# Fewer and larger weight loads, weight reductions behind the attention group, and memory loads issued after the stage before them

## The reference

```python
q, k, v = x @ w_q.T, x @ w_k.T, x @ w_v.T
sigma_q = elu(q) + 1
a_mem = einsum('bsd,mde->mbse', sigma_q, memories)
raw   = einsum('bsd,md->mbs', sigma_q, memory_norms)
w     = softmax(raw.mean(axis=-1), axis=0)
mem_out = einsum('mbse,mb->bse', a_mem / clip(raw, 1e-6)[..., None], w)
out = g * mem_out + (1 - g) * causal_attention(q, k, v)      # 16 heads of 128
x = layernorm(x + out @ w_o.T)
h = relu(bitlinear(x, w_up)) ** 2                            # 2048 -> 4096
x = layernorm(x + bitlinear(h, w_down))                      # 4096 -> 2048
```

## Time and profile before

| | |
|---|---|
| median of 3 runs | 3046.87 us (3042.25 to 3052.11) |
| the profiled execution | 3053.26 us |
| its span on the slowest core (core 7) | 3051.7 us |
| spans of the eight cores | 3004.0 to 3051.7 us |
| TensorE busy / VectorE / ScalarE / GpSimd | 74% / 37% / 23% / 9% of the span |
| read from memory / written | 294.23 MB / 8.39 MB |

### The profile page before, as it was taken

The page is one execution under the profiler, slowest core; times in us unless marked ns, Lnnn a source line. Parts: engine busy times, 40 slices in busy tenths (PEclk is TensorE's granted clock), DMA queues, the critical chain, the costliest instruction groups (busy, mean ns, idle before and its releaser), DMA issues.

```text
span 3051.7 us, 37968 instructions; the slowest of 8 cores (3004.0 to 3051.7 us)
## 1 busy us (share of the span) xinstructions
PE 2263.3 (74%) x14858; PEld 1450.8 (48%) x14858; DVE 1136.6 (37%) x1393; ACT 713.5 (23%) x1232; POOL 287.2 (9%) x453
## 2 busy tenths in 40 slices
PE   0299799898988988960999999496347992445883
PEld 0044353452543534510888888142236881334673
DVE  0043313323233233254111111545336765655444
ACT  0011123323323223242011111032322222441221
POOL 4100130211211201001100100000000000000000
PEclk9999899999999999975999999598558996777997
DMA  8700251533433425217374660264002532103322
GB/s 110 111 1 1 44 88 56 111 97 69 92 89 97 83 65 122 63 42 82 42 98 57 81 87 1 33 128 116 28 1 90 159 111 83 56 1 108 114 84 111
DMA packets 194597, 229.58 MB, mean 75 GB/s; under 512 B 15091, under 2 KB 162548, under 8 KB 193396
## 3 DMA queue, kind: packets, MB, share of 16 engines
q0 software_dynamic: 134160, 109.10, 23.3%
q1 hardware_dynamic: 59108, 109.66, 11.8%
q10 hardware_dynamic: 1152, 8.39, 0.7%
HBM read 294.23 MB, written 8.39 MB: 99 GB/s over the span
## 4 chain that ended last, share of the span: by engine, by line
PE 66%; DVE 15%; DMA 9%; issue 3%; ACT 3%; POOL 2%; DVEq 1%; ACTq 0%; POOLq 0%; SPq 0%
PE ps_all L777 15%; PE ps_all L482 8%; PE ps_all L462 7%; PE ps_all L316 7%; PE ps_all L1128 7%; PE ps_all L1323 6%; PE ps_all L534 4%; PE ps_all L529 3%; PE ps_all L989 2%; PE ps_all L552 2%; DMA wfd<-wdnT 2%; DVE wdb L1286 2%; DMA membuf<-mem 2%; DMA wqb<-wqT 1%; DMA xTb<-xT 1%
## 5 line engine op out<-in xcount | busy, mean ns | idle before, releaser
L777 PE MATMUL ps_all<-membuf,sigT 128*128 128x256 bf16 x4096 | 450.0, 273 | 41.3 <-DMA membuf<-mem 41.3
L777 PEld LDWEIGHTS ps_all<-membuf,sigT 128*128 128x128 bf16 x4096 | 402.0, 98 | 89.1 <-issue 41.4
L1323 PE MATMUL ps_all<-wdb,rtq 128*128 128x256 bf16 x2048 | 254.5, 292 | 97.8 <-DVE wdb L1286 56.4
L316 PE MATMUL ps_all<-xTb,wqb 128*128 128x512 bf16 x1024 | 222.9, 381 | 136.6 <-DMA wqb<-wqT 136.6
L1323 PEld LDWEIGHTS ps_all<-wdb,rtq 128*128 128x128 bf16 x2048 | 212.9, 104 | 139.3 <-issue 101.4
L1128 PE MATMUL ps_all<-wub,xqT 128*128 128x256 bf16 x2048 | 251.9, 289 | 26.5 <-DVE wub L1069 13.1
L1128 PEld LDWEIGHTS ps_all<-wub,xqT 128*128 128x128 bf16 x2048 | 209.9, 103 | 67.2 <-issue 33.0
L482 PE MATMUL ps_all<-vw,xTb 128*128 128x256 bf16 x2048 | 229.9, 276 | 12.4 <-DVE lsT L430 12.4
L462 PE MATMUL ps_all<-xTb,kw 128*128 128x512 bf16 x1024 | 224.6, 382 | 18.6 <-DMA kw<-wkT 18.6
L302 DVE TENSOR_REDUCE swpart<-swst 128x1 f32<-128x1024 f32 x128 | 153.7, 1216 | 193.0 <-DMA swst<-wupT 103.0
L316 PEld LDWEIGHTS ps_all<-xTb,wqb 128*128 128x128 bf16 x1024 | 100.5, 98 | 258.5 <-issue 139.0
(11 more groups left out here) (160 smaller groups left out, 2157.9 us busy)
## 6 DMA issues: line engine op xcount, KB each, us to landing
swst<-wupT SPq DMA_DIRECT2D x64, 512.0 KB, 4.6
swst<-wdnT SPq DMA_DIRECT2D x64, 512.0 KB, 4.4
membuf<-mem POOLq DMA_DIRECT2D x64, 512.0 KB, 19.2
wfs<-wupT POOLq DMA_DIRECT2D x16, 1024.0 KB, 7.2
wfs<-wupT SPq DMA_DIRECT2D x16, 1024.0 KB, 6.9
wfd<-wdnT SPq DMA_DIRECT2D x16, 1024.0 KB, 7.0
wfd<-wdnT POOLq DMA_DIRECT2D x16, 1024.0 KB, 6.8
xTb<-xT POOLq DMA_DIRECT2D x64, 128.0 KB, 8.2
```

Source lines behind the costliest of these rows:

```text
L316: k.emit("tensor", lambda t, oc=oc, lc=lc, dc=dc, bank=bank: t.matmul(ps[bank][:, 0:CH], wqb[:, dc * D + oc * 128: dc * D + (oc + 1) * 128 ...
L777: k.emit("tensor", lambda t, ss=ss, m=m, dc=dc, bank=bank, buf=buf: t.matmul(ps[bank][:, 0:256], sigT[:, dc * OWN + ss * 128: dc * OWN + ( ...
L1323: k.emit("tensor", lambda t, ss=ss, ic=ic, bank=bank, buf=buf: t.matmul(ps[bank][:, 0:256], rtq[:, qbase(ss) + ic * 128: qbase(ss) + ic * ...
```

## The change

- `wqb` comes in one transfer instead of 16.
- `kw` and `vw` come in one transfer each per head pair instead of 16 each. Their rows are then taken sixteen blocks at a time: "(c p) w -> p c w".
- The four `emit_swjob2` of a group are emitted behind the group's matmuls and behind the finish of the group before, instead of ahead of them.
- The loads of `membuf` are four transfers of 2048 rows instead of eight of 1024. The first two loads, which were emitted ahead of the fence that ends B0 and waited for `sigT` alone, are emitted behind it with the others.
- `dn_t[0]` is set behind all cells of the column blocks 0 and 1, after the flush.

```diff
-        for dc in range(NCK):
-            k.emit("gpsimd", lambda g, dc=dc: g.dma_start(
-                wqb[:, dc * D:(dc + 1) * D],
-                wqT.ap()[dc * 128:(dc + 1) * 128, :]),
-                waits=k.ch(gld) if dc == 0 else (), inc=gld, inc_k=16)
+        k.emit("gpsimd", lambda g: g.dma_start(
+            wqb[:].rearrange("p (c w) -> p c w", w=D),
+            wqT.ap().rearrange("(c p) w -> p c w", p=128)),
+            waits=k.ch(gld), inc=gld, inc_k=16)
...
-            for dc in range(NCK):
-                k.emit("gpsimd", lambda g, hp=hp, dc=dc: g.dma_start(
-                    kw[:, dc * 256:(dc + 1) * 256],
-                    wkT.ap()[dc * 128:(dc + 1) * 128,
-                             hp * 256:(hp + 1) * 256]),
-                    waits=([(tmm, kw_t)] + k.ch(s_kv)) if dc == 0 else (),
-                    inc=s_kv, inc_k=16)
+            k.emit("gpsimd", lambda g, hp=hp: g.dma_start(
+                kw[:].rearrange("p (c w) -> p c w", w=256),
+                wkT.ap()[:, hp * 256:(hp + 1) * 256].rearrange(
+                    "(c p) w -> p c w", p=128)),
+                waits=[(tmm, kw_t)] + k.ch(s_kv), inc=s_kv, inc_k=16)
...
                 for o in range(2):
-                    for _ in range(4):
-                        if swq:
-                            emit_swjob2(swq.pop(0))
                     plist = pairs_by_o[o]
...
                         emit_group_fin(finq.pop(0))
                     att_t = tmm.n
                     gidx += 1
+                    for _ in range(4):
+                        if swq:
+                            emit_swjob2(swq.pop(0))
...
+        endphase()
...
-        def emit_memload(et, extra=()):
-            buf = et % 2
-            for m in range(M4):
-                for dq in range(2):
-                    c0 = (m * NCK + dq * 8) * 256
...
-        b0_e = ch["e"][NCK - 1]
-        emit_memload(0, extra=[(vve, sigT_v), (sse, b0_e)])
-        emit_memload(1, extra=[(vve, sigT_v), (sse, b0_e)])
-        endphase()
...
         for et in range(8):
             buf = et % 2
-            if et >= 2:
-                emit_memload(et)
-            mld = mld_et[et]
+            for m in range(M4):
+                c0 = m * NCK * 256
+                k.emit("gpsimd", lambda g, et=et, m=m, buf=buf, c0=c0: g.dma_start(
+                    membuf[buf][:, c0:c0 + NCK * 256].rearrange(
+                        "p (c w) -> p c w", w=256),
+                    mem.ap()[m * D:(m + 1) * D,
+                             et * 256:(et + 1) * 256].rearrange(
+                        "(c p) w -> p c w", p=128)),
+                    waits=([(tmm, mem_t[buf]), (sdbg, dbg_gate0)]
+                           + k.ch(s_me[buf]) if m == 0 else ()),
+                    inc=s_me[buf], inc_k=16)
+            mld = s_me[buf].n
+            k.chend(s_me[buf])
...
             emit_c4_mm(0, ss)
-            if ss == 7:
-                dn_t[0] = tmm.n
             if ss >= 1:
                 emit_c4_mm(1, ss - 1)
         emit_c4_mm(1, 7)
+        flush_cells()
+        dn_t[0] = tmm.n
         dn_t[1] = tmm.n
-        flush_cells()
```

More of the change, by code:

```diff
@@ L438, in build_program @@
         for hp in range(8):
-            for dc in range(NCK):
-                k.emit("gpsimd", lambda g, hp=hp, dc=dc: g.dma_start(
-                    kw[:, dc * 256:(dc + 1) * 256],
-                    wkT.ap()[dc * 128:(dc + 1) * 128,
-                             hp * 256:(hp + 1) * 256]),
-                    waits=([(tmm, kw_t)] + k.ch(s_kv)) if dc == 0 else (),
-                    inc=s_kv, inc_k=16)
+            k.emit("gpsimd", lambda g, hp=hp: g.dma_start(
[3 more added lines that the diff above has]
+                waits=[(tmm, kw_t)] + k.ch(s_kv), inc=s_kv, inc_k=16)
             kld = s_kv.n
             k.chend(s_kv)
[L448 to L454, removed]
+            k.emit("gpsimd", lambda g, hp=hp: g.dma_start(
+                vw[:].rearrange("p (c w) -> p c w", w=256),
+                wvT.ap()[:, hp * 256:(hp + 1) * 256].rearrange(
+                    "(c p) w -> p c w", p=128)),
+                waits=[(tmm, vw_t)] + k.ch(s_kv), inc=s_kv, inc_k=16)
             vld = s_kv.n
@@ L731, in build_program @@
         dbg_gate0 = sdbg.n
+        endphase()
         membuf = [ov.tensor(f"membuf{i}", [128, M4 * NCK * 256], BF16, 4, 4)
                   for i in range(2)]
+        memtok = ov.tensor("memtok", [128, 8 * D], BF16, 4, 5)
         mem_t = [a2_t, a2_t]
-        mld_et = {}
-        def emit_memload(et, extra=()):
-            buf = et % 2
-            for m in range(M4):
-                for dq in range(2):
-                    c0 = (m * NCK + dq * 8) * 256
[L743 to L754, removed]
-        b0_e = ch["e"][NCK - 1]
-        emit_memload(0, extra=[(vve, sigT_v), (sse, b0_e)])
-        emit_memload(1, extra=[(vve, sigT_v), (sse, b0_e)])
-        endphase()
-        memtok = ov.tensor("memtok", [128, 8 * D], BF16, 4, 5)
         ev_v = 0
```

## The result

The changed kernel takes 3064.81 us (median of 10 runs) against 3045.79 us for the kernel before (10 runs): a ratio of 1.0067, 95% interval 1.0050 to 1.0083, so +20 us (15 to 25). Forecast were 3065.0 us and +18.1 us.

What follows compares the result with a forecast made beforehand. TensorE's row of stages was taken to bound the kernel, with holes waiting for loads or VectorE. +0.7 - 4 + 7.8 + 13.6 = +18.1 us on the median 3046.87 gave 3065.0 us; 3046 to 3080 for 8 in 10.

Steps and rivals of the forecast that it cites:

- Query weights, +0.7 us: Load before the first query matmul: one transfer is issued later than a first piece was, +0.7 us (-3 to +13).
- rival 3: Row order, sixteen blocks 1 MB apart, slows query and memory loads: about +35 us, 3082 us; chance 0.08.
- Key weights, -4 us: First key load, the only one waited for: one transfer fills idle DMA time and takes a larger share, -4 us (0 to -10).
- the idle 30% during the issue: First key load: DMA share was 0.70 during GpSimd's 7.8 us of issuing; one transfer can fill the rest, 2.3 us.
- Reductions, +7.8 us: End of attention: four reductions now delay the last finish, +7.8 us (+7 to +9); hidden at the head-pair boundaries.
- Memory loads, +13.6 us: Before the first memory matmul: issue 13.2 us later behind the fence, first issue 0.4 us longer; +13.6 us (+5 to +18).
- the contention is the same: First memory load: the second again follows at once, both buffers in flight, so contention is unchanged; the load took 52.9 us.
- Rival 1: The straggling first memory load shrinks by ten us, sum +8 us, 3055 us, lost in noise; chance 0.18.
- Guard, 0: FFN down: the ternarisation waiting on dn_t[0] already stands behind those cells' sums, 0; without that cover 3.01 + 0.48 us.
- The signs named beforehand: Memory idle about 55 us, start +18; issue behind last coefficient operation; four reductions between last finishes; key wait 14; query start 137.
- the three signs of being wrong: Memory load length changes over 10 us; a later key, value or memory load is waited for; mid-head-pair stalls change.
- Rivals 2 and 4: 2: coalesced first loads drain faster, -17 us, 3030, chance 0.07; 4: moved reductions hidden, +10 us, 3057, chance 0.05.

Runs made afterwards that it cites:

- e3: Kernel before with query, key and value loads as single transfers and each memory load as four, memory loads still early: 0.9985 (0.9966 to 1.0004).
- e8: Changed kernel with eight reductions behind the last group but one and none behind the last: 1.0057 (1.0041 to 1.0074) against the kernel before.
- e9: Changed kernel with the last group's four reductions emitted behind the finish after the last key matmuls: 1.0018 (0.9999 to 1.0036) against the kernel before.
- e11: Kernel before with four reductions ahead of the finish after the key matmuls, twelve behind, second memory load after the first, all loads coalesced: 0.9705, 2962.1 us.
- e7: Kernel before with sixteen reductions at a time behind the finish after the key matmuls and second memory load after the first: 0.9828, two executions.
- e2: Kernel before with only the four reductions of a group moved behind its matmuls and the finish before it: 1.0060 (1.0027 to 1.0093).
- e1: Kernel before with only the first two memory loads emitted behind the fence, still eight transfers each: 1.0050 (1.0029 to 1.0072).
- e4: Kernel before with only the guard dn_t[0] set behind all cells of the first two column blocks: 3040.2 and 3045.1 us, no ratio.
- e12: Kernel before with four reductions ahead of the finish after the key matmuls, twelve behind, second memory load after the first, loads not coalesced: 0.9725 (0.9691 to 0.9759).
- e6: Kernel before with the second memory load made to wait until the first has landed: 0.9964 (0.9948 to 0.9981).

## Why the prediction was right

- **Query weights, +0.7 us:** 54.3 against 53.6 us from issue to first matmul. Over the kernels with one transfer (changed, e3, e8, e9, e11) the mean idle time is 135.8 us, over the others but e7 135.6. The DMA engines were full during it, the number of transfers made no difference, and the row order does not hurt: rival 3, with up to +13 us here, falls. The rule on row pitches that stood beside it, the Trainium skill's "DMA: Bandwidth & Descriptors", section "Latency and other measured facts", is measured there on copies from the sync and scalar queues, with the pitch from partition to partition. In this load, which GpSimd issues, the 1 MB step lies between the blocks of one partition, so this case neither bears its figures out nor speaks against them.
- **Key weights, -4 us:** mis-sized. The same two groups of kernels have 14.9 and 16.3 us: -1.4 us. The step that was too large is the gain from the idle 30% during the issue and from a larger share beside the other queue. That the engines were already full for the 12.5 us behind it, as the text said, is the likely reason; no run tried it without the other queue. The estimate of 6.8 us from the Trainium skill, "DMA: Bandwidth & Descriptors", section "Anatomy of one DMA", stands against 19.5 us in the changed kernel; its -13.5 us did not come.
- **Reductions, +7.8 us:** +9.3 us on the mean in the changed kernel, +9.8 in e2. The mechanism, its place and the hiding at the seven boundaries were as written; the block measured elsewhere (7.8 us) was 1 us shorter than the one that came (8.9).
- **Memory loads, +13.6 us:** the delay of the issue alone is worth 13.4 us (e1). What failed is the step "the contention is the same" with +0.4 us for larger transfers: they made the load shorter by 5.0 us over ten profiles, by 2.2 in that of the change, so the term came to +11.4 us there and to +8.4 by the means. Rival 1 had this mechanism, with 10 us for it where 5 came.
- **Guard, 0:** nothing in e4 moves.
- **Sum of the idle times:** by the means +0.2 - 1.4 + 9.3 + 8.4 = +16.5 us; by the changed kernel's own profile +1.8 - 0.7 + 9.3 + 11.4 = +21.8 us; measured +20 us (15 to 25). The forecast of +18.1 is closer than its terms deserve: two gains were mis-sized in opposite directions (2.6 us too much for the keys, 5 us too little for the memories) and the reductions by 1.5 us too little. That 3064.81 lies within 1 us of the 3065.0 forecast is luck: the interval alone is 10 us wide.
- **Sum of the times:** e1, e2 and e3 measured alone add up to +0.95%, or +29 us, with intervals that reach from about +16 to +42 us. They hold the +20 us and do not sharpen it: the account rests on the idle times.
- **The signs named beforehand:** on core 7 the idle time before the first memory matmul went from 41.3 to 51.9 us (55 forecast) and its start from 1455.67 to 1474.51 (+18.8, 18 forecast). The four reductions and the place of the memory issue came as written. The wait for the first key load did not fall to about 14 us: 18.6 to 17.0 us on core 7, 16.3 to 15.6 on the mean. Of the three signs of being wrong none came: the memory load changed by 2.2 us on the mean, no later load is waited for, and the stalls in the middle of the head pairs are 5.1 to 6.7 us in the changed kernel where they were 5.0 to 6.2.
- **Rivals 2 and 4** fall: no gain passed 27 us, and the moved reductions were not hidden at the end.

What stays open: why four transfers of 2048 rows bring the same bytes sooner than eight of 1024. Whether it still holds when one load runs alone is not shown: e11 with four pieces has 31.3 us, and of the kernels with eight e12 has 34.8 and e6 32.9. Whether it is the shorter issue (4.57 us for four, 7.0 for eight) or something in the transfers was not tried. Open too is what the two cores of a pair share when both load the memories.

## What to carry to other kernels

A prefetch that is moved behind a fence costs about the distance to the fence (13.4 us of idle time for 13.2 here) if the consumer is already waiting for it, and a transfer started beside it on the same engines can stretch it by a third (42.7 against 32.9 us): start the second when the first has landed. Work that an in-order engine does on the side belongs where the critical engine is busy for longer than the side work takes at the pace of its loads, not at the pace of its arithmetic. When adding up idle time to see what a stall is worth, add the slower matmuls behind it.

## What the runs showed of the hardware

- A wait of TensorE of 5 to 6 us, eight times, cost not only its 47 us of idle time but about 25 us of matmuls at the lower clock behind it: mean granted clock 0.60 in the 10 us from 1327 us on, where the stall ends at 1327.49, 1.00 before it and 11 us after it.
- The first of two queued memory loads took 42.7 us on the mean with the second in flight, 27 to 53 us over the cores, and 32.9 us without. In all 56 pairs of cores the one that issued first had the shorter load.
- GpSimd's issue of the last part of the second load stood still until the first load had landed, with eight pieces (1455.93 us) and with four (1470.40 us), although the fifteen and seven before it had gone out at once.
